# A residual product by subject on one core: the ring of x holds eight tiles in place of twelve

## The reference

```python
w = weights[subjects]                       # (128, 128, 128)
out = jnp.einsum('bct,bcd->bdt', x, w)      # (128, 128, 1024)
return x + out
```

## Time and profile before

| | |
|---|---|
| median of three runs | 323.97 us |
| the profiled execution's own time | 323.31 us |
| its span, first to last instruction | 321.5 us |
| mean granted TensorE clock | 0.938 of full speed |
| TensorE matmul, busy | 243.8 us |
| VectorE, busy | 196.3 us |
| ScalarE, busy | 132.2 us |
| moved by DMA | 134.83 MB, mean 419 GB/s |

### The profile page before, as it was taken

The page is one execution under the profiler, slowest core; times in us unless marked ns, Lnnn a source line. Parts: engine busy times, 40 slices in busy tenths (PEclk is TensorE's granted clock), DMA queues, the critical chain, the costliest instruction groups (busy, mean ns, idle before and its releaser), DMA issues.

```text
span 321.5 us, 2871 instructions
## 1 busy us (share of the span) xinstructions
PE 243.8 (76%) x1024; PEld 112.7 (35%) x1024; DVE 196.3 (61%) x261; ACT 132.2 (41%) x131; POOL 0.8 (0%) x7
## 2 busy tenths in 40 slices
PE   0799997878687866779868698666986868876650
PEld 0344442334343432334424244333333434443320
DVE  3288888637657555764757737567463774755560
ACT  4056566324444242542425525335342553443450
POOL 1000000000000000000000000000000000000000
PEclk9999999979989997997979979998897998999995
DMA  7999999999999999999999999999999999999996
GB/s 287 422 411 427 421 428 425 428 429 429 425 428 428 428 426 428 428 427 427 428 429 428 426 427 430 428 425 428 430 427 426 426 431 428 426 425 432 421 428 271
DMA packets 18024, 134.83 MB, mean 419 GB/s; under 512 B 1105, under 2 KB 1633, under 8 KB 1633
## 3 DMA queue, kind: packets, MB, share of 16 engines
q1 hardware_dynamic: 9232, 67.64, 50.2%
q10 hardware_dynamic: 8784, 67.12, 49.4%
HBM read 67.64 MB, written 67.11 MB: 419 GB/s over the span
## 4 chain that ended last, share of the span: by engine, by line
DMA 73%; PE 17%; DVE 3%; issue 3%; DVEq 1%; ACT 1%; ACTq 0%
DMA out<-x_ring 37%; DMA x_ring<-x 34%; PE product L222 17%; DVE x_ring L140 2%; DMA weight_halves<-weights 1%; ACT weight_bank L174 1%; DVE x_ring L139 1%; DVEq L53 0%; DVEq L124 0%; DVEq L132 0%; DVE weight_bank L119 0%; DVE weight_ring L132 0%; ACTq L188 0%; DVEq L153 0%
## 5 line engine op out<-in xcount | busy, mean ns | idle before, releaser
L222 PE MATMUL product<-x_ring,weight_ring 64*128 64x512 f32 x1024 | 243.8, 630 | 66.1 <-DMA x_ring<-x 43.2
L222 PEld LDWEIGHTS product<-x_ring,weight_ring 64*128 64x128 f32 x1024 | 112.7, 199 | 196.4 <-issue 123.2
L139 DVE TENSOR_TENSOR x_ring<-product,x_ring 64x1024 f32<-64x1024 f32 x64 | 77.9, 1217 | 106.6 <-PE product L222 106.6
L182 ACT COPY x_ring<-product 64x1024 f32<-64x1024 f32 x64 | 64.5, 1008 | 175.5 <-PE product L222 175.5
L140 DVE TENSOR_TENSOR x_ring<-product,x_ring 64x1024 f32<-64x1024 f32 x64 | 78.6, 1228 | 0.8
L183 ACT COPY x_ring<-product 64x1024 f32<-64x1024 f32 x64 | 64.2, 1003 | 0.8
L132 DVE COPY weight_ring<-weight_bank 64x256 f32 x128 | 36.9, 288 | 3.9 <-issue 1.0
L174 ACT COPY weight_bank<-weight_halves 64x1024 f32<-64x1024 f32 x2 | 2.2, 1115 | 2.1 <-DMA weight_halves<-weights 2.1
L144 DVE TENSOR_SCALAR subject_row<-subject_row 1x128 int32<-1x128 int32 x1 | 0.2, 215 | 3.6 <-DMA subject_row<-subjects 3.6
L113 DVE COPY weight_bank<-weight_halves 64x1024 f32<-64x1024 f32 x2 | 1.4, 688 | 0.9 <-DMA weight_halves<-weights 0.9
L174 ACT ACT_TABLE_LOAD x1 | 1.3, 1283 | 1.3 <-PEq L240 1.3
## 6 DMA issues: line engine op xcount, KB each, us to landing
x_ring<-x SPq DMA_DIRECT2D x32, 2048.0 KB, 22.0
out<-x_ring ACTq DMA_DIRECT2D x29, 2048.0 KB, 26.2
out<-x_ring ACTq DMA_DIRECT2D x6, 1024.0 KB, 10.6
weight_halves<-weights SPq DMA_DIRECT2D x1, 512.0 KB, 3.9
subject_row<-subjects ACTq DMA_DIRECT2D x1, 8.0 KB, 2.8
```

Of the source, the lines that this page charges most:

```text
L139: dve.tensor_tensor(x_ring[LOW, slot, 0, :], low[LOW, :], x_ring[LOW, slot, 0, :], add)
L182: act.copy(x_ring[LOW, slot, 1, :], low[HIGH, :])
L222: last = pe.matmul(product[slot % PRODUCTS][a][:, cols], weight_ring[half, slot, r, :], x_ring[half, slot, r, cols], start=r == 0, stop=r ...
```

## The change

The ring has eight slots, four places of one pair, and `weight_ring` has eight slots as well. 64 tiles are then eight laps of eight, REST is 0, and the code behind TensorE's loop goes. A new constant LAST = 4 keeps the last four tiles single, so that SINGLE is as before. SyncE's waits for a landed load (LOADS_AHEAD) are gone: the first four loads go out without a wait, and from the fifth on each waits for the stores of its place. The number of tiles, the DMAs, their sizes and the work of each tile are the same.

```diff
--- before.py
+++ after.py
@@ -5,11 +5,11 @@
 
 PSUM_BANK_COLS = 512
 DMA_INC = 16
-SLOTS = 12
+SLOTS = 8
 PAIR = 2
-LOADS_AHEAD = 4
 PICK_AHEAD = 4
 PRODUCTS = 2
+LAST = 4
 
 
 def subject_residual_kernel(nc, x, subjects, weights, out):
@@ -29,12 +29,12 @@
     H, R = C // 2, 2
     TILES = B // 2
     LAPS, REST = divmod(TILES, SLOTS)
-    assert LAPS and SLOTS % PRODUCTS == 0 and REST % PRODUCTS == 0 and REST == PICK_AHEAD > PRODUCTS
+    assert REST == 0 and SLOTS % PRODUCTS == 0 and SLOTS >= 2 * PICK_AHEAD and PICK_AHEAD > PRODUCTS
     PAIRS, PAIR_SLOTS = TILES // PAIR, SLOTS // PAIR
-    assert SLOTS % PAIR == 0 and REST % PAIR == 0 and LOADS_AHEAD < PAIR_SLOTS
+    assert SLOTS % PAIR == 0 and LAST % PAIR == 0
     BANKS = T // PSUM_BANK_COLS
 
-    SINGLE = (*range(PAIR), *range(TILES - REST, TILES))
+    SINGLE = (*range(PAIR), *range(TILES - LAST, TILES))
 
     SUBJECT_ROWS = 16
 
@@ -93,8 +93,6 @@
                 lap, place = divmod(pair, PAIR_SLOTS)
                 if lap:
                     sp.wait_ge(x_out[place], stores(lap, place) * DMA_INC)
-                elif place >= LOADS_AHEAD:
-                    sp.wait_ge(x_in[place - LOADS_AHEAD], DMA_INC)
                 sp.dma_start(x_ring[:, place * PAIR:(place + 1) * PAIR, :, :], x_of_pair[pair]).then_inc(x_in[place], DMA_INC)
 
         @block.gpsimd
@@ -205,7 +203,7 @@
                     act.dma_start(out_of_pair[tile // PAIR], x_ring[:, place * PAIR:(place + 1) * PAIR, :, :]).then_inc(
                         x_out[place], DMA_INC)
             for place in reversed(range(PAIR_SLOTS)):
-                act.wait_ge(x_out[place], DMA_INC * stores(LAPS + (place < REST // PAIR), place))
+                act.wait_ge(x_out[place], DMA_INC * stores(LAPS, place))
 
         @block.tensor
         def _(pe):
@@ -229,8 +227,6 @@
             with pe.Fori(0, LAPS) as lap:
                 for slot in range(SLOTS):
                     multiply(lap * SLOTS + slot, slot, lap * DMA_INC + DMA_INC)
-            for slot in range(REST):
-                multiply(LAPS * SLOTS + slot, slot, DMA_INC * (LAPS + 1))
 
 
 def kernel(x, itok_B_0_7, L0_cond_weights):
```

## The result

The changed kernel takes 327.83 us (median of six runs, 326.81 to 329.68), the kernel before 323.82 us beside it (323.25 to 324.35): a ratio of 1.0133, 95% interval 1.0114 to 1.0151. Forecast were 328.0 us.

The account below looks back on a forecast made before the run. The prediction took the 16 DMA engines to bound the kernel. Middle 0, start 1.5 and end 2.5 us sum to 4.0, on 323.97 giving 328.0 us; the 8-in-10 range was 324.3 to 332.7.

Parts of the forecast that it names:

- The bound and the turn: Whole kernel: DMA engines set the time; with four places a turn must fit into 39.2 us, so the middle costs 0.
- sum of a turn: One place from load to free again, without queues: 30.4 us needed, against 39.2 with four places and 29.4 with three.
- rival of unshortened transfers: Middle: load and store times of 22 and 27 us are latency, a turn stays 59.6 us, 476 us in all; chance 0.02.
- dry middle: Middle: a queue empties and refills in each pair, 8 to 17 us more, or 4 in a milder case; chance 0.17.
- lead of 4 us: Middle: each next transfer is issued some 4 us or more before its queue runs out, so the engines stay fed.
- The start: Start: engines run out at 28.9 us, before pair 1's store and load 4 bring data; 1.5 us lost, bounds 0.4 to 4.1.
- first store's low stretch (365): From 22 to 24 us, as the first store joined the loads: 365 GB/s in place of 428, 0.3 us lost.
- TensorE's wait of about 4 us: Start: TensorE, done with pair 3 at 37.9, waits some 4 us for load 4, off the path.
- The end: End: gaps before the last two stores, formerly covered by the backlog of stores, cost 2.5 us, bounds 1.0 to 4.6.
- gap before tile 62: End: the store queue empties before tile 62's store has data flowing, 1.4 us; tile 62 is issued 6.4 us after the last landing.
- The first byte: Each gap: 1.1 us from issue to first data, taken as 1.5 with the ramp; with the skill's 600 ns the sum is about 1.3.
- Not slower: End: DMA engines that are behind catch up in the gaps, 2.4 us come back, 323.0 with gaps at lower bounds; chance 0.14.

Follow-up runs that it names:

- ring10: The kernel before with a ring of ten slots (five places of a pair), nothing else changed: 324.09 us, ratio 1.0008 to the kernel before.
- ring6: The kernel before with a ring of six slots (three places) and LOADS_AHEAD = 2: 369.79 us, ratio 1.1404 to the kernel before.
- w_mid: The kernel before, ring of twelve; only the loads of pairs 8 to 23 wait for the store four pairs back: 324.50 us, ratio 1.0028.
- fix_start: The changed kernel with pair 4 loaded in two single tiles, the first once tile 0 has been stored: 328.22 us, ratio 1.0123 to the kernel before.
- w_all: The kernel before, ring of twelve; all loads from the fifth on wait for the store four pairs back: 327.23 us, ratio 1.0128.
- end_split: The changed kernel with the last pair loaded in two single tiles, each with its own semaphore: 325.74 us, ratio 1.0053 to the kernel before.
- w_start: The kernel before, ring of twelve; only loads 4 and 5 wait, for the stores of pairs 0 and 1: 326.64 us, ratio 1.0093.
- single8: The changed kernel with PAIR = 1, eight places of one tile: 324.71 us, ratio 1.0019 to the kernel before.

## Why the prediction was right, and where its terms were off

**The bound and the turn** held. The DMA engines set the time, transfers shortened by as much as their queues (14.1 and 15.1 us against the 15 and 15 forecast), and the middle costs next to nothing in the changed kernel: 428 GB/s from 100 to 200. ring10 and ring6 put the edge between three and four places, where the sum of a turn had it. The rival of unshortened transfers is out, and so is the dry middle as a loss in each pair. But the lead of 4 us that the prediction gave each transfer isn't what protects the middle. After 50 us one of the changed kernel's queues ran empty eight times, for 0.8 to 1.5 us, which is the rival's condition; the other queue took the whole rate, and no such time cost over 0.2 us. In w_mid and fix_start some did cost 0.5 us and more, so the 0 is this kernel's measurement and no rule.

**The start**, put at 1.5 us, is worth more. The gap itself came as drawn: data end at about 29, the store goes out at 29.70, and the two stretches lose 1.3 us. What the sum lacked is the 1.0 us after it, when load 4 has been issued beside the running store and the store's packets slow down to 279 GB/s, and that it can be 3.1 us if the load goes first. The first store's low stretch (365) had shown such a cost, and I used it for a rival alone. Measured: 2.3 us in the changed kernel's trace, 2.0 in that of w_all, 1.7 us left over in end_split, 3.0 us in w_start. TensorE's wait of about 4 us came (4.31 us, from 40.8), but by two errors that cancel: it was done with pair 3 at 40.8 and not 37.9 (by its own row, a store issued at 43.06 less 2.6 for the eviction, the prediction should have had 40.5), and load 4 landed at 45.1, not 41.1. The fifth slice's drop (367) was not forecast.

**The end**, put at 2.5 us, measured 2.1 to 2.6 by end_split. The gap before tile 62 was sized with TensorE at full clock; in the profiled execution tile 62's store came 8.1 us after the landing in place of 6.4, and the trace of before had such a pair in it (8.72 us), which I called hidden. That holds in the middle, not for the last pair. The last store came 11.5 us after the last landing, 1.6 later than forecast. The backlog was shorter too: the rate falls soon after 316, about 5 us after the landing at 311.4, where the sum had 6.4.

w_all's profile has the same waits with TensorE at full clock. Its windows of the end:

```profile
316.00:318.00 2.00, 2.00 (x10) 0.68 (x7) 1.19 (x1) 0.75 (x1) 0.00 (x0) 1.00 0.21 86
...
320.00:322.00 2.00, 0.00 (x0) 0.00 (x0) 0.62 (x1) 0.19 (x1) 0.00 (x0) 1.00 0.61 254
...
324.00:325.10 1.10, 0.00 (x0) 0.00 (x0) 0.00 (x0) 0.00 (x0) 0.00 (x0) 0.50 0.01 0
```

The two gaps lose 1.6 and 0.8 us, together the 2.4 that was forecast (1.4 and 1.0). But the tail behind them is short: 1.2 us are missing from 322 on, against 2.9 from 318 on before. So from 316 on w_all loses only 0.9 us more than the kernel before, and the changed kernel's profiled execution, with gaps of 4.6 us (316 to 324) and a tail of 1.1, 2.7 more.

**The first byte**: the store issued at 29.70 has no packet up to 30.5 and 23 of them from there to 31, the first at 30.6. That is 0.9 us with nothing else running, a little under the row's 1.1. The Trainium skill's 600 ns ("DMA: Bandwidth & Descriptors", "Latency and other measured facts") is less than either, and the sum by it, an estimate of 1.3 us, is a third of the 4.0 measured.

**Not slower** failed for the whole, but its mechanism is there at the end. The last store of before has its 16 increments, which I take for one from each DMA engine, spread over 2.6 us (318.4 to 320.9); in w_all and in the changed kernel (326.6 to 326.8) they come within 0.2 us. So the engines that are behind do catch up in the gaps, and the tail is 1.7 and 1.9 us shorter, near the 2.4 that the rival had put on it. The gaps are larger than that, so the kernel is slower.

That the sum met the measured time within 0.2 us is partly luck. The start was too small by 0.2 to 1.5 us. At the end the sum had neither the slow last pair nor the shorter tail, which work against each other; by the traces the end costs 0.9 to 2.7 us, by end_split 2.1 to 2.6.

## What to carry to other kernels

As far as this case shows, in a kernel bound by DMA a ring may shrink for as long as its turn without queues (own transfers at the shared rate, landings, compute at the clock it will have) fits into places times the period; then the middle is all but free and the cost lies at the start and the end, where a place comes free late and a backlog is short. Both grow with the size of one transfer: places of half the size bought back most of it here (single8), a last load cut in two over half (end_split). Part of a gap at the end comes back, since the DMA engines that are behind catch up in it. Past the edge TensorE's clock falls too and lengthens the turn, as one profile shows (ring6).

## What was not expected of the hardware

Two queues that start at about the same time get in each other's way. In w_start load and store were issued 0.07 us apart, and until 33 only loads had packets, at 49 to 74 GB/s between 30 and 32. In the changed kernel, with the store 0.37 us ahead, the load's packets came 4.4 us after its issue, and before they came the store's own packets slowed down: 279 GB/s from 32 to 34 at a DMA share of 1.02. So the share alone does not tell whether the engines lose time; the GB/s beside it do.
